# Window attention on one core: one value slot in place of two, value eviction on VectorE, and a new order of MLP input, residual sum and fourth maximum on VectorE and GpSimd

## The chip, the cores and the metric

The kernel runs on 1 core of one Trainium2 chip. The metric is the device time of one execution in microseconds (us). Three executions of the kernel before took 1966.45, 1970.64 and 1970.95 us; the median is 1970.64 us.

## The reference

Two layers work on x, float32 of shape 8 x 48 x 112 x 112. The change touches the first alone: attention in shifted windows of 7 x 7 tokens, 3 heads of 16 channels, then an MLP of 192 hidden channels.

```python
xn = layernorm(x over channels); xs = roll(xn, (-3, -3))
xw = xs as windows of 49 tokens                       # 2048 windows
q, k, v = split(xw @ qkv_w + qkv_b)                   # 3 heads of 16
attn = softmax(q @ k.T * 16 ** -0.5 + bias)
out = (attn @ v) @ proj_w + proj_b
x = x + roll(out back to the image, (3, 3))
h = gelu(layernorm(x) @ fc1_w + fc1_b)
x = x + (h @ fc2_w + fc2_b)
```

The second layer (a 7 x 7 depthwise convolution, a normalisation, an MLP with a response norm and a residual) follows in the same launch. Its code is the same before and after.

## The kernel before

**Tiling.** `attention_phase` goes through 64 strips. A strip is two rows of 16 windows, one on partitions 0 to 48, one on partitions 64 to 112: 784 columns of 48 channels and a row of ones. A strip's attention is done in 4 quads (j = 0 to 3) of 4 windows of each partition half, so 8 windows together.

**Keys, values and scores.** `u_product` multiplies a strip's normalised input with each head's query-key matrix; the result `Uf` (float32) and its low part `Ul` (bf16) hold, in `UV` slots of 784 columns, three heads and behind them the value weights. `keys_and_values` (L931) then uses the tokens of a window as weights and lets the slots of `Uf` and `Ul` pass: one product gives a window's 3 x 49 scores and its values in one row of PSUM tile `ps_t`, `SV` = 49 `UV` columns. Before, `UV` is 5: two slots hold the value weights, once with the columns of the upper half and once with those of the lower (`wv`, `wv_swap`), so that 96 value columns come out with zeros in place of the other half's channels. `key_bias` (L944) and `shift_scores` (L959) add the bias and subtract the maximum.

**Eviction.** On ScalarE, `exp_scores` (L716) writes the exponentials of a quad to `P` and `keep_values` (L725) copies its value columns to `V`, 113 x 384 at a time; both have two buffers. `weigh` (L973, L978) multiplies `P` with `V` and with ones, `invert_sums` (L733) and `invert_sums_end` (L740) give the reciprocals of the sums, and `divide` (L522, VectorE) writes `O`. `project` (L987) multiplies `O` with `proj_w`.

**After attention.** `first_residual` (L533, VectorE) adds the input and gives `x1`, in two halves; `x1_low` (L441, GpSimd) takes its low part; `centre` (L848) sums the channels, `subtract_mean` (L543), `square`, `variance` (L848), `log_variance` and `root` give the scale; `normalise1` (L551, VectorE) gives `xh1`, the MLP's input, `low1` (L406, GpSimd) its low part. `fc1` (L1009) in three parts, `gelu` (ScalarE) and `fc2` (L1022, L1028) follow, and `second_residual` (L563, VectorE) writes the result.

**Order.** Each engine runs a list written out by hand, `step(s)`, that mixes four strips: `s` (attention), `prv` = s - 1 (last quads, projection, first residual), `old` = s - 2 (MLP), and `nxt`, `nx2` (input). Semaphores count what is done. TensorE's order in a step is: quad 0 of `keys_and_values`, `variance(old)`, `weigh(prv, 3)`, `u_product(nxt, 0)`, quad 1, `project(prv)`, `weigh(s, 0)`, `u_product(nxt, 1)`, quad 2, `u_product(nxt, 2)`, `weigh(s, 1)`, `centre(prv)`, quad 3, `fc1(old, 0..2)`, `weigh(s, 2)`, `fc2(old)`, with the query scores of later quads between them.

**Banks.** Projection, centring, `u_product`, `fc1` and `fc2` share the three banks of `ps_m`. `BANKS` says which: `"proj": (1, 2)`, `("u", 1): (0, 1)`, `("u", 2): (2, 0)`. So `u_product(nxt, 1)` writes bank 1, which `project(prv)` filled just before, and waits until the first half of `first_residual(prv)` has read it; `u_product(nxt, 2)` waits so for the second half.

```python
mm(bank("proj", b)[0:R, 0:HALF], proj_w[:], O[:, s.slot(2), cols_of(b)],
   start=True, stop=True).then_inc(S["proj"], 1)
taken("proj", b, S["x1_made"], 2 * s.n + b + 1)
```

**Start.** Ahead of the first strip ScalarE spreads the value weights over both rings of `Uf` in eight copies (L800), and GpSimd takes their low parts in two instructions of 1568 columns (L460). `keys_and_values` of the first quad waits for these.

## Time and profile before

| | before |
|---|---|
| three executions, median | 1970.64 us |
| profiled execution, its own time | 1975.34 us |
| its span, first to last instruction | 1973.7 us |
| TensorE busy | 1772.9 us, 90% |
| ScalarE busy | 1541.7 us, 78% |
| VectorE busy | 1365.0 us, 69% |
| GpSimd busy | 1170.0 us, 59% |
| mean granted TensorE clock | 0.951 |

The span has three stretches: the attention phase from the start to about 1378 us, the convolution to about 1625 us, the second MLP to the end. The profiled execution took 4.70 us more than the median of the three; 1.64 us of its time lie outside the span. Busy shares are means over the whole span, so what bounds the attention phase has to be read from the timeline of one strip. In a timeline row an instruction's successor on the same engine often starts some 0.08 us before the recorded end.

### The profile page before, as it was taken

To read this page: it belongs to the slowest core of one execution; us is meant where nothing else is said; L and a number is where in the kernel's file an instruction comes from. 1 tells how busy PE (TensorE), PEld (TensorE's weight loads), DVE (VectorE), ACT (ScalarE), POOL (GpSimd) and SP (SyncE) were. 2 spreads that over 40 slices of the span, in tenths; PEclk is the share of its full clock that TensorE was granted. 3 is DMA by queue.
4 is the path that set the end of the run, shared out by engine and by line. 5 is a ranking of instruction groups with operands and counts; after the bars stand their busy time and mean duration, and the time that the engine had idled before them with its cause. 6 is when DMAs were issued, how large, how long until landed. Compare 5 with 4: busy or idle time off the path is not lost. (4 is left out here: it accounts for less than half of the span.)

```text
span 1973.7 us, 90330 instructions
## 1 busy us (share of the span) xinstructions
PE 1772.9 (90%) x38186; PEld 1076.4 (55%) x38186; DVE 1365.0 (69%) x2016; ACT 1541.7 (78%) x2904; POOL 1170.0 (59%) x1048
## 2 busy tenths in 40 slices
PE   4999999999999999999999998995899967999996
PEld 2666556656565565655666565651497943333332
DVE  7776666767676676766767676642777766888883
ACT  3788788888888788888888888873766647888882
POOL 5687686777778677777877777652255550122222
PEclk9999999999999899999999999996799985999998
DMA  4344554444444344444444444411488759999994
GB/s 111 94 108 99 139 129 103 105 102 110 100 113 102 96 107 100 116 99 105 106 107 103 104 112 99 98 45 43 109 216 216 214 135 170 227 253 253 262 258 147
DMA packets 233228, 262.26 MB, mean 133 GB/s; under 512 B 167079, under 2 KB 179911, under 8 KB 232711
## 3 DMA queue, kind: packets, MB, share of 16 engines
q1 hardware_dynamic: 217478, 217.50, 46.2%
q0 software_dynamic: 15360, 39.08, 6.6%
q8 instruction: 304, 4.98, 1.1%
q14 instruction: 86, 0.70, 0.1%
HBM read 160.82 MB, written 80.88 MB: 122 GB/s over the span
## 5 line engine op out<-in xcount | busy, mean ns | idle before, releaser
L416 POOL TENSOR_TENSOR shift<-const_b,qmax 113x588 bf16<-113x588 bf16 x256 | 299.4, 1170 | 231.8 <-DVE qmax L511 230.1
L563 DVE TENSOR_TENSOR x<-ps_m,x 112x392 f32<-112x392 f32 x128 | 66.5, 561 | 272.8 <-PE ps_m L1028 272.8
L511 DVE TENSOR_REDUCE qmax<-ps_s 113x12 f32<-113x588 f32 x256 | 194.9, 761 | 66.8 <-PE ps_s L907 66.7
L1487 POOL DMA_DIRECT2D out_rolled<-r_OUT x128 | 63.8, 503 | 270.2 <-DVE r_OUT L1587 270.2
L716 ACT ACTIVATE P<-ps_t 113x588 f32<-113x588 f32 x256 | 172.0, 672 | 58.4 <-PE ps_t L959 57.1
L748 ACT ACTIVATE G<-ps_m 128x392 f32<-128x392 f32 x384 | 178.3, 500 | 46.0 <-PE ps_m L1009 45.5
L503 DVE TENSOR_TENSOR Ul<-Uf 113x784 bf16<-113x784 f32 x192 | 208.5, 1113 | 0.0
L1333 PE MATMUL conv_ps<-xin,band_now 64*64 64x448 bf16 x2688 | 203.1, 364 | 2.2 <-DVE x_low L1228 2.2
L406 POOL TENSOR_TENSOR xhl<-xh 113x784 bf16<-113x784 f32 x64 | 200.7, 3137 | 2.2 <-DVE xh L551 2.2
L709 ACT COPY Uf<-ps_m 113x392 f32<-113x392 f32 x384 | 172.9, 486 | 33.0 <-PE ps_m L874 24.8
L1333 PE MATMUL conv_ps<-x_low,band_now 64*64 64x448 bf16 x1344 | 179.6, 351 | 0.0
L973 PEld LDWEIGHTS ps_o<-P,V 113*32 113x32 f32 x6144 | 109.1, 110 | 99.3 <-ACT P L716 53.0
L522 DVE TENSOR_TENSOR O<-ps_o,rden 96x196 f32<-96x196 f32 x256 | 90.0, 352 | 89.5 <-ACT rden L740 84.0
L1333 PEld LDWEIGHTS conv_ps<-xin,band_now 64*64 64x64 bf16 x2688 | 136.2, 105 | 22.9 <-issue 3.9
L973 PE MATMUL ps_o<-P,V 113*32 113x49 f32 x6144 | 143.2, 211 | 4.2 <-issue 0.6
L441 POOL TENSOR_TENSOR xl<-x 113x784 bf16<-113x784 f32 x64 | 137.0, 2141 | 12.1 <-DVE x L533 7.0
L733 ACT ACTIVATE lden<-ps_o 96x196 f32<-96x196 f32 x256 | 84.5, 330 | 74.4 <-PE ps_o L978 65.8
L978 PE MATMUL ps_o<-P,pack 113*32 113x98 f32 x3072 | 136.6, 250 | 0.1
L1201 POOL DMA_DIRECT2D y_scratch<-y x96 | 67.9, 708 | 112.6 <-ACT y L1272 105.9
L389 POOL TENSOR_TENSOR t_cen<-XT,t_mean 112x672 f32<-112x672 f32 x64 | 126.3, 1973 | 10.9 <-DVE t_mean L482 10.9
L1624 ACT ACTIVATE r_G<-r_ps_f 128x784 f32<-128x784 f32 x128 | 104.6, 839 | 28.5 <-PE r_ps_f L1694 28.4
L725 ACT COPY V<-ps_t 113x384 f32<-113x384 f32 x256 | 125.0, 488 | 1.9 <-PE ps_t L959 1.9
(244 smaller groups left out, 5203.9 us busy)
## 6 DMA issues: line engine op xcount, KB each, us to landing
xin<-rows_scratch SPq DMA_DIRECT2D x96, 236.0 KB, 3.8
XT<-x_tokens SPq DMA_DIRECT2D x64, 294.0 KB, 3.3
X<-x_windows SPq DMA_DIRECT2D x128, 147.0 KB, 3.4
RS<-rs_scratch SPq DMA_DIRECT2D x128, 147.0 KB, 3.4
XR<-x_windows SPq DMA_DIRECT2D x128, 147.0 KB, 3.2
x_scratch<-x SPq DMA_DIRECT2D x128, 147.0 KB, 3.4
y_scratch<-y POOLq DMA_DIRECT2D x96, 196.0 KB, 2.9
r_RS<-rs_scratch SPq DMA_DIRECT2D x128, 147.0 KB, 4.6
```

The source lines that it names most:

```text
L389: nc.gpsimd.tensor_tensor(t_cen[:].rearrange("p (t c) -> p t c", c=C), XT[:, s.slot(2), :].rearrange("p (t c) -> p t c", c=C), mean, ALU.s ...
L406: nc.gpsimd.tensor_tensor(xhl1[:], xh1[:], xm1[0], ALU.subtract).then_inc(S["lo1"], 1)
L416: nc.gpsimd.tensor_tensor(shift[:, j % 2], e, m, ALU.mult).then_inc(S["md"], 1)
L441: nc.gpsimd.tensor_tensor(xl1[:], x1[:, r, :], x1m[0][:, r, :], ALU.subtract).then_inc(S["x1_lo"], 1)
L503: nc.vector.tensor_tensor(Ul[:, r, h, :], Uf[:, r, h, :], U[0][:, r, h, :], ALU.subtract).then_inc(S["u_lo"], 1)
L511: nc.vector.tensor_reduce(qmax[:, j % 2, :].rearrange("p (b n) -> p b n", b=2), ps_s[0:R, :, 0:2 * HQ].rearrange("p b (n t) -> p b n t", t ...
L709: nc.scalar.copy(Uf[:, s.slot(2), h, cols_of(b)], bank(("u", h), b)[0:R, 0:HALF]).then_inc(S["u_hi"], 1)
L716: nc.scalar.activation(P[:, j % 2].rearrange("p (b n) h t -> p b n (h t)", b=2), ps_t[0:R, :, 0:2 * SV].rearrange("p b (n c) -> p b n c", ...
L748: nc.scalar.activation(out, bank(("f1", k), b)[:, 0:HALF], ACT.Gelu).then_inc(S["ge"], 1)
L973: mm(ps_out[lo:lo + 2 * DH, TOK * k:TOK * k + TOK], V[:, j % 2, k, lo:lo + 2 * DH], P[:, j % 2, k, h, :], start=True, stop=True)
L978: ins = mm(ps_den[lo:lo + 2 * DH, 2 * TOK * b:2 * TOK * (b + 1)], key_ones[:, b ^ j // 2, :], P[:, j % 2, 2 * b:2 * b + 2, h, :], start=Tr ...
L1333: ins = mm(ps[s][SIDE * k:SIDE * k + SIDE, side, 0:half * IMG], band_now[lo:lo + SIDE, s, w, t, :], part[lo:lo + SIDE, s, half * k:half * ...
```

## The change

1. `UV` becomes `HEADS + 1`. One slot holds the value weights of both halves, so the moving side of each L931 product is 4 x 49 = 196 columns and no longer 245. `wv_swap` goes; the setup copies to `Uf` become two, of 784 columns, and GpSimd's low parts two of 784.
2. A product now gives 48 value columns for each half, without zeros. `V` is laid out as [row, quad parity, window, channel, half]; VectorE evicts a quad with two copies of 49 partitions x 192 columns, one for each half of the partitions, each writing every second word. The places of the other half are cleared once, on GpSimd. ScalarE's four `keep_values` in a strip go.
3. The copies of quads 0 and 1 wait for ScalarE's exponentials of the same quad, those of quads 2 and 3 come first and the exponentials wait for them.
4. For quads 2 and 3 the windows of a quad are taken in another order, and `O` and `proj_w` are laid out to fit: `project` makes two products as before, of windows by kind and not by half, and `first_residual` reads and writes 4 x 98 columns in place of 392 running ones.
5. VectorE's order: `normalise1(old)` moves ahead of `first_residual(prv)`, `query_max(s, 3)` behind it, and the four `keep_values` are put in. GpSimd's order: `low1(old)` goes ahead of `x1_low(prv)`, and `make_shift(s, 3)` behind both.

```diff
-        UV = HEADS + 2
+        UV = HEADS + 1
...
-        V = sb("V", [R, 2, QP, 2 * C])
+        V = sb("V", [R, 2, QP, C, 2])
...
-        O = sb("O", [2 * C, 2, STRIP])
+        O = sb("O", [2 * C, 2, 2, QUADS, 2 * TOK])
...
+        def kept_values(p, j):
+            lo = ROWB * p
+            to = V[lo:lo + TOK, j % 2, :, :, p].rearrange("p (b k) c -> p b k c", b=2)
+            of = ps_t[lo:lo + TOK, :, 0:2 * SV].rearrange("p b (k c) -> p b k c", c=SV)[:, :, :, HQ:HQ + C]
+            return to, of
...
                 make_shift(s, 2)
+                low1(old)
+                x1_low(prv)
                 make_shift(s, 3)
-                x1_low(prv)
-                low1(old)
...
+            def keep_values(s, j):
+                if s.real:
+                    q = 4 * s.n + j
+                    wait(dve, S["st"], q + 1)
+                    if j < QUADS // 2:
+                        wait(dve, S["ex"], q + 1)
+                    wait(dve, S["pv"], q - 1)
+                    for p in range(2):
+                        nc.vector.tensor_copy(*kept_values(p, j)).then_inc(S["vev"], 1)
...
                 query_max(s, 2)
+                keep_values(s, 0)
                 token_sums(s.at(4))
                 token_squares(s.at(3))
                 divide(prv, 3)
                 normalise0(nx2)
+                normalise1(old)
+                keep_values(s, 1)
+                first_residual(prv)
                 query_max(s, 3)
-                first_residual(prv)
-                normalise1(old)
                 divide(s, 0)
+                keep_values(s, 2)
...
                 divide(s, 1)
+                keep_values(s, 3)
                 query_max(nxt, 1)
...
             def exp_scores(s, j):
...
+                    if j >= QUADS // 2:
+                        wait(act, S["vev"], 2 * (q + 1))
...
-                                    w = QP * j + 2 * b + k
+                                    w = QP * j + 2 * (b ^ j // 2) + k
```

VectorE in a step, from the division of quad 2 of `prv` to that of quad 0 of `s` (`L522` before, `L542` after; `L533` and `L553` are the first residual, `L551` and `L572` `normalise1`, `L534` the new copies). Before:

```order
L522 TENSOR_TENSOR O<-ps_o,rden 96x196
L511 TENSOR_REDUCE qmax<-ps_s 113x12
L479 TENSOR_REDUCE t_sum<-XT 112x14
L482 TENSOR_SCALAR t_mean<-t_sum 112x14
L488 TENSOR_REDUCE t_var<-t_sqr 112x14
L522 TENSOR_TENSOR O<-ps_o,rden 96x196
L497 TENSOR_TENSOR xh<-X,RS 113x784
L511 TENSOR_REDUCE qmax<-ps_s 113x12
L533 SCALAR_TENSOR_TENSOR x<-ps_m,out_b,XR 113x392 x2
L551 SCALAR_TENSOR_TENSOR xh<-xc,centred_b,rs 113x784
```

The same place after:

```order
L520 TENSOR_REDUCE qmax<-ps_s 113x12
L534 COPY V<-ps_t 49x192 x2
L488 TENSOR_REDUCE t_sum<-XT 112x14
L491 TENSOR_SCALAR t_mean<-t_sum 112x14
L497 TENSOR_REDUCE t_var<-t_sqr 112x14
L542 TENSOR_TENSOR O<-ps_o,rden 96x2x98
L506 TENSOR_TENSOR xh<-X,RS 113x784
L572 SCALAR_TENSOR_TENSOR xh<-xc,centred_b,rs 113x784
L534 COPY V<-ps_t 49x192 x2
L553 SCALAR_TENSOR_TENSOR x<-ps_m,out_b,XR 113x4x98 x2
L520 TENSOR_REDUCE qmax<-ps_s 113x12
```

Ahead of the first residual two pairs of copies and `normalise1` are new, and the fourth maximum has gone behind it.

GpSimd from the shift of quad 3 on (`L416`, after `L425`; `xhl` is written by `low1`, `xl<-x` by `x1_low`). Before:

```order
L416 TENSOR_TENSOR shift<-const_b,qmax 113x588 x2
L441 TENSOR_TENSOR xl<-x 113x784
L406 TENSOR_TENSOR xhl<-xh 113x784
L389 TENSOR_TENSOR t_cen<-XT,t_mean 112x672
L416 TENSOR_TENSOR shift<-const_b,qmax 113x588
```

After:

```order
L425 TENSOR_TENSOR shift<-const_b,qmax 113x588
L415 TENSOR_TENSOR xhl<-xh 113x784
L450 TENSOR_TENSOR xl<-x 113x784
L425 TENSOR_TENSOR shift<-const_b,qmax 113x588
L398 TENSOR_TENSOR t_cen<-XT,t_mean 112x672
L425 TENSOR_TENSOR shift<-const_b,qmax 113x588
```

The low part of the MLP's input now comes first, that of the residual sum second, and the fourth shift third.

## Rows read from the trace of the kernel before

**Rows 1.** Timeline of TensorE, one strip: start us, us, line, output and inputs, count.

```profile
910.65 0.30 PE L931 MATMUL ps_t<-Uf,xh 49*49 49x245 bf16 x4
...
911.72 0.33 PE L907 MATMUL ps_s<-swap,Uf 49*49 49x49 bf16 x24
911.88 0.42 PE L959 MATMUL ps_t<-shift,const_b 49*49 49x294 bf16 x4
...
915.96 1.57 PE L987 MATMUL ps_m<-O,pack 96*113 96x392 f32 x4
...
918.28 0.36 PE L874 MATMUL ps_m<-xh,gram_h 49*49 49x392 bf16 x4
...
921.56 0.38 PE L848 MATMUL ps_m<-x,sum_w 113*113 113x392 bf16 x1
...
922.12 0.33 PE L848 MATMUL ps_m<-xl,sum_w 113*113 113x392 bf16 x1
922.40 0.30 PE L931 MATMUL ps_t<-Uf,swap 49*49 49x245 bf16 x4
...
923.48 0.32 PE L907 MATMUL ps_s<-xh,Uf 49*49 49x49 bf16 x24
923.77 0.37 PE L1009 MATMUL ps_m<-xh,w_part_h 49*64 49x392 bf16 x4
...
926.84 0.35 PE L1009 MATMUL ps_m<-xh,w_own_h 49*128 49x392 bf16 x2 [0.52 <-ACT G L748]
...
930.74 0.30 PE L931 MATMUL ps_t<-Uf,xh 49*49 49x245 bf16 x4
```

**Rows 2.** Timeline of VectorE in the same strip.

```profile
912.87 0.84 DVE L479 TENSOR_REDUCE t_sum<-XT 112x14 f32<-112x672 f32 x1
...
914.14 0.84 DVE L488 TENSOR_REDUCE t_var<-t_sqr 112x14 f32<-112x672 f32 x1
915.09 0.36 DVE L522 TENSOR_TENSOR O<-ps_o,rden 96x196 f32<-96x196 f32 x1
915.37 0.96 DVE L497 TENSOR_TENSOR xh<-X,RS 113x784 f32<-113x784 f32 x1
...
917.02 1.18 DVE L533 SCALAR_TENSOR_TENSOR x<-ps_m,out_b,XR 113x392 f32<-113x392 f32 x2
918.12 1.03 DVE L551 SCALAR_TENSOR_TENSOR xh<-xc,centred_b,rs 113x784 f32<-113x784 f32 x1
...
924.47 0.76 DVE L511 TENSOR_REDUCE qmax<-ps_s 113x12 f32<-113x588 f32 x1
```

**Rows 3.** Timeline of ScalarE in the same strip.

```profile
912.34 0.66 ACT L716 ACTIVATE P<-ps_t 113x588 f32<-113x588 f32 x1 [0.68 <-PE ps_t L959]
...
919.07 0.87 ACT L709 COPY Uf<-ps_m 113x392 f32<-113x392 f32 x2
```

**Rows 4.** Timeline of GpSimd in the same strip.

```profile
918.34 2.15 POOL L441 TENSOR_TENSOR xl<-x 113x784 bf16<-113x784 f32 x1
920.46 3.26 POOL L406 TENSOR_TENSOR xhl<-xh 113x784 bf16<-113x784 f32 x1
```

**Rows 5.** Groups of instructions: count, busy us, mean ns of one, idle before.

```profile
L1515 DVE COPY r_w1t<-r_ps_f 48x192 f32<-48x192 f32 x1 | 0.3, 342 | 0.0
L563 DVE TENSOR_TENSOR x<-ps_m,x 112x392 f32<-112x392 f32 x128 | 66.5, 561 | 272.8 <-PE ps_m L1028 272.8
L725 ACT COPY V<-ps_t 113x384 f32<-113x384 f32 x256 | 125.0, 488 | 1.9 <-PE ps_t L959 1.9
```

**Rows 6.** GpSimd's `squares_low` (L433), all 64: duration ns min/median/max.

```profile
L433 POOL TENSOR_TENSOR sql<-sq x64: 1485/1489/1498, 71.2 to 1347.7; 113x784 bf16<-113x784 f32 x64
```

**Rows 7.** Timeline of the start: GpSimd, then VectorE.

```profile
26.10 8.01 POOL L460 TENSOR_TENSOR Ul<-Uf 113x1568 bf16<-113x1568 f32 x2 [3.87 <-ACT Uf L800]
...
30.49 6.46 DVE L503 TENSOR_TENSOR Ul<-Uf 113x784 bf16<-113x784 f32 x3
```

**Rows 8.** One stretch of 20 us: busy us (count) of PE, PEld, DVE, ACT, POOL; PEclk, DMA.

```profile
220.00:240.00 20.00, 17.95 (x397) 10.85 (x399) 11.97 (x17) 13.62 (x30) 12.48 (x11) 0.83 0.38 106
```

More of the change, by code:

```diff
@@ L530, in first_residual @@
                     wait(dve, S["x2_made"], 2 * (s.n - 1))
-                    for b in range(2):
-                        wait(dve, S["proj"], 2 * s.n + b + 1)
+                    for a in range(2):
+                        wait(dve, S["proj"], 2 * s.n + a + 1)
                         nc.vector.scalar_tensor_tensor(
-                            out=x1[:, r, cols_of(b)], in0=bank("proj", b)[0:R, 0:HALF], scalar=out_b[:, 0:1],
-                            in1=XR[:, r, cols_of(b)], op0=ALU.add, op1=ALU.add).then_inc(S["x1_made"], 1)
+                            out=of_kind(x1[:, r, :], a), in0=bank("proj", a)[0:R, 0:HALF].rearrange("p (j t) -> p j t", j=QUADS),
+                            scalar=out_b[:, 0:1], in1=of_kind(XR[:, r, :], a), op0=ALU.add, op1=ALU.add
+                            ).then_inc(S["x1_made"], 1)
             def subtract_mean(s):
@@ L797, in _ @@
             for r in range(2):
[L798 to L803 removed]
+                nc.scalar.copy(Uf[:, r, HEADS, :].rearrange("p (w t) -> p w t", t=TOK),
+                               wv[:].unsqueeze(1).to_broadcast([R, WINS, TOK])).then_inc(values_spread, 1)
             steps(step, -1, N + 2)
@@ L922, in keys_and_values @@
                     wait(pe, S["ex"], q)
-                    wait(pe, S["vev"], q)
+                    wait(pe, S["vev"], 2 * q)
                     r = s.slot(2)
@@ L984, in project @@
                     wait(pe, S["nrm"], 4 * s.n + 4)
-                    for b in range(2):
-                        free_m("proj", b)
-                        mm(bank("proj", b)[0:R, 0:HALF], proj_w[:], O[:, s.slot(2), cols_of(b)],
+                    for a in range(2):
+                        free_m("proj", a)
+                        mm(bank("proj", a)[0:R, 0:HALF], proj_w[:, a, :], O[:, s.slot(2), a],
                            start=True, stop=True).then_inc(S["proj"], 1)
-                        taken("proj", b, S["x1_made"], 2 * s.n + b + 1)
+                        taken("proj", a, S["x1_made"], 2 * s.n + a + 1)
             def fc1(s, k):
@@ L1790, in constants @@
             minus[lo + j, j] = -1
-    key_ones = np.zeros((R, 2, 2 * DH), f)
+    key_ones = np.zeros((R, DH, 2), f)
     for g in range(2):
@@ L1794, in constants @@
         ones[lo:lo + TOK, lo:lo + TOK] = 1
-        for b in range(2):
-            key_ones[lo:lo + TOK, b, DH * (g ^ b):DH * (g ^ b) + DH] = 1
+        key_ones[lo:lo + TOK, :, g] = 1
     out["picks"] = np.concatenate([pick, ones, minus], 1)
-    out["key_ones"] = key_ones.reshape(R, 4 * DH)
+    out["key_ones"] = key_ones.reshape(R, 2 * DH)
     out["eye"] = np.eye(128, dtype=f)
@@ L1859, in packs_of @@
         put(a, PACK_A, "w2_part", prm0["fc2_w"][F1:HID], F2 * g)
-        for h in range(HEADS):
-            put(a, PACK_A, "proj_w", prm0["proj_w"][DH * h:DH * h + DH], 2 * DH * h + DH * g, lo)
+        for kind in range(2):
+            first = PACK_A["proj_w"].start + R * kind + ROWB * (g ^ kind)
+            a[g:2 * C:2, first:first + C] = prm0["proj_w"]
         put(a, PACK_A, "bias", by_query, lo)
```

56 lines of the change are left out of this document (19 added, 37 removed).

## The prediction

> **What bounds the kernel now.** I read the engines' totals first, then the timeline of one strip, engine by engine, then the groups of instructions. The totals name TensorE, but a mean says little; in the timeline the same strip comes back every 20.09 us, from one L931 to the next, 910.65 to 930.74 [rows 1]. Below, times are counted from 910.65. TensorE is the engine that sets the end, and the reader is to see in its rows where it runs product behind product and where it waits. It waits for the GELU in the MLP (0.52 at 16.19, and once more like it). It also waits twice by little: the last centring product starts at 11.47, its successor could start 0.17 later, yet L931 starts at 11.75, 0.11 late (behind an exponential); and the 24 score products of L907 take 0.16 at 1.07 but 0.29 at 12.83, because the MLP behind them waits for GpSimd's low part, which ends at 923.72 and lets L1009 start at 923.77 [rows 1, 4]. All else around the change hangs on this list, so I ask of each edit whether it moves a product of TensorE.
>
> **Fewer columns.** From 910.65 to 911.72 TensorE does six groups of 245 columns and three of 294, 2352 columns in 1.07 us, 0.455 ns each [rows 1]. So 49 columns less in six groups save 0.13 us a quad, 0.53 a strip, if columns are all that counts; if the groups are held by something else, nothing. I take 0.13 and keep 0 for the range. Only what no later wait eats is a gain.
>
> **ScalarE** loses 4 copies of 0.49 us a strip, 125 us in all [rows 5]. It gains TensorE nothing by itself: where ScalarE is waited for, it has itself waited for TensorE just before (0.68 us ahead of the exponential of quad 0 [rows 3], and in the GELU part the chain goes product, GELU, product). I count 0.
>
> **VectorE's copies.** No row shows this copy. The nearest is a copy of 48 x 192 out of PSUM, 342 ns [rows 5]. Since a successor starts 0.08 before the recorded end (0.36 at 915.09, successor at 915.37 [rows 2]), a pair costs 0.54 us; 2.2 us a strip, on an engine that was busy for 69% of the span. What matters is where they stand. Two pairs and `normalise1` come ahead of the first residual, the maximum goes behind it. Walk VectorE with its old durations [rows 2, 3]. The exponential of quad 0 ended at 2.35; 0.13 earlier is 2.22, and VectorE's token sums began at 2.22 as well. First pair from 2.26, token sums at 2.80 (old 2.22), squares 1.27 later at 4.07, division 0.76 later at 4.83 (old 4.44), `normalise0` at 5.11, `normalise1` 0.88 later at 5.99, second pair 0.95 later at 6.94, first residual at 7.48 (old 6.37). Its first half takes 0.63 (the pair took 1.18, so one starts 0.55 after the other): 8.11.
>
> The division's end, 5.19, lets the projection start at about 5.3, where it started before (5.31): the saving of quads 0 and 1, 0.26, is gone there. Then the bank: `u_product(nxt, 1)` started at 7.63 [rows 1] and had slack, since the residual's first half was done at 7.0. Now it starts at 8.11 and 0.1 for the signal (GpSimd to TensorE took 0.05 above): 8.21, **0.58 late**. This is a new wait, TensorE for VectorE. Behind it hang ScalarE's two copies of that product, at 8.42 before [rows 3], then the reciprocal, the division of quad 0, the second `weigh`; they were already one chain from product to centring, so centring is as late, 11.49, and the columns of quad 2 are covered by that chain.
>
> **From centring on.** Its four products take 0.73 without the old wait of 0.11 (ScalarE's exponential of quad 2 no longer stands behind a copy): L931 of quad 3 at 12.22. From there to the MLP it was 1.37; less 0.13 of columns and 0.13 of waiting for GpSimd: 1.11, so 13.33 (old 13.12). What follows to the end of the strip, 6.97, goes by GELU and stays. A strip would be 20.30. One thing more is late: VectorE came to the next strip's first maximum at 13.82 and comes to it some 1.4 later; it ends near 16.0, and the last third of `fc1`, behind scores that wait for it, wants to start at 16.4. I add 0.08 for it (0 to 0.4). **Sum: +0.29 us a strip**, over 63 strips +18.
>
> **GpSimd's order.** `low1` took 3.26 and `x1_low` 2.15, `squares_low` of the same shape always 1.49 [rows 4, 6]. The first two lie over VectorE instructions with two inputs in SBUF. `low1` now starts at about 7.1 beside copies out of PSUM; at 1.49 it ends at 8.6, `x1_low` starts at 8.8 and ends at 10.3, ahead of the centring at 11.5. So the gain is the 0.13 counted above. By the Trainium skill, "SBUF — State Buffer", section "SBUF: two separate sides", whichever of GpSimd and a VectorE instruction with two SBUF inputs starts first holds the shared ports for its whole length. The trace agrees (3.26 against 1.49). By that rule the three L503 subtractions would now run into the fourth shift and the token centring, which is one more reason for the 0.08.
>
> **Start.** GpSimd's 8.01 us for the value weights' low parts become two of about 1.5 to 2.5, and VectorE's three subtractions, 6.46 us for what takes 0.9 each elsewhere, are free of it [rows 7]. I take -4 us once (-2 to -5). Setup rows that go otherwise hide under this. The convolution and the second MLP: 0.
>
> The profiled execution took 1975.34, 4.7 above the median, and the sum of changes applies to either: 1975.3 + 18 - 4 = 1989 for it, and 1970.6 + 14 = 1985 for the median.
>
> **Rivals.** (A) As worked out: 1975 to 1998, with the columns worth 0 (+0.13 twice, +16 us) at the upper end and shorter copies at the lower.
>
> (B) The copies are slower: they write every second word, which no row of VectorE shows. Bound: a copy of 192 that costs what 392 elements cost, 561 ns [rows 5], is 0.22 longer; four of them stand ahead of the first residual: +0.88 a strip, +55, 2040. Half of that gives 2012. Against it: all PSUM reading rows here lie near one element a cycle. By the Trainium skill, "Vector Engine (DVE) Microarchitecture Reference", section 5.2, a stream is at full rate only in runs of two adjacent words, and a destination that hops every element measured 1.71 ns an element against 1.054; by its figures an estimate is 0.13 a copy, +0.5 a strip and 2018. No run here shows it yet.
>
> (C) It comes out faster. Mechanism: VectorE reaches the first residual at or before 6.9, so that the bank is free at 7.63, and TensorE runs at its own pace: centring at 10.9, L931 at 11.65, MLP at 12.76, strip 19.73, -0.36 and -23, with the start 1944. It decides at 0.58 us off VectorE's stretch from 0.3 to 8.1; that is the price of the two pairs less one copy, or 0.2 off each of the three long instructions that I walked at their old durations. For it: no row shows the copies, and my walk carries three signals at 0.04 to 0.1 each. Against: the other terms of the walk are rows.
>
> (D) A wash: half of the new wait, and the start's gain: 1965 to 1976.
>
> (E) The clock. In one stretch of 20 us it was granted at 0.83 with TensorE busy for 17.95 [rows 8]; at full clock that work would take 3 us less (17.95 x 0.17). A new wait of 0.6 us in each strip may make such stretches more or fewer; three of them either way are 10 us. It has no chance of its own and widens all cases.
>
> **How the numbers follow.** Chances: A 0.50, B 0.17, C 0.20, D 0.13. The likeliest gives 1985; its own range is 1975 to 1998. The range for 8 in 10 leaves out the lower half of C and the upper third or so of B: 1950 to 2022. About 0.3% (6 us) is what a measurement of this kernel can tell from no change. Slower by more than that: A and B, 0.66 with a little of A given to no change; same: most of D, 0.13; faster: C and a rest of D, 0.21.
>
> **What would show it.** Right: strips of about 20.3 to 20.4; L874 of the second product preceded by idle time that ends with VectorE's first residual, 0.5 us a strip; copies at about 0.34; `low1` at about 1.5; the first L931 some 4 us earlier. Wrong: copies of 0.45 or more (B), or no wait of TensorE for the residual and a strip under 20 (C); L931 groups no shorter than before, which costs A 0.13 to 0.26 a strip; or the MLP's last part waiting for a maximum, which would make the 0.08 larger.

## The result, and the profile after

| | before | after |
|---|---|---|
| median of the executions taken side by side | 1968.55 us (4) | 2209.46 us (4) |
| range | 1965.45 to 1970.95 | 2200.37 to 2212.59 |
| span of the profiled execution | 1973.7 us | 2210.9 us |
| TensorE busy | 1772.9 us | 1893.0 us |
| VectorE busy | 1365.0 us | 1567.9 us |
| ScalarE busy | 1541.7 us | 1453.9 us |
| GpSimd busy | 1170.0 us | 981.4 us |
| mean granted TensorE clock | 0.951 | 0.881 |

The changed kernel takes 1.1222 times as long, 95% interval 1.1186 to 1.1257. The prediction, 1985 us with 2022 as its upper end, had the sign right and missed the size by a factor of about 17: +241 us and not +14.

Timeline of TensorE after, one strip of 24.57 us, from one L938 (it was L931) to the next; columns as in [rows 1].

```profile
906.68 0.27 PE L938 MATMUL ps_t<-Uf,xh 49*49 49x196 bf16 x4
906.78 0.26 PE L938 MATMUL ps_t<-Ul,xh 49*49 49x196 bf16 x4
...
912.01 1.57 PE L996 MATMUL ps_m<-O,pack 96*113 96x392 f32 x4 [0.21 <-DVE O L542]
...
915.25 0.36 PE L881 MATMUL ps_m<-xh,gram_h 49*49 49x392 bf16 x4 [0.85 <-DVE x L553]
...
918.53 0.38 PE L855 MATMUL ps_m<-x,sum_w 113*113 113x392 bf16 x1
...
919.34 0.28 PE L938 MATMUL ps_t<-Uf,swap 49*49 49x196 bf16 x4
...
922.14 0.37 PE L1018 MATMUL ps_m<-xh,w_part_h 49*64 49x392 bf16 x4 [1.51 <-DVE xc L564]
...
923.87 0.56 PE L1018 MATMUL ps_m<-xhl,w_own_h 49*128 49x392 bf16 x2
...
928.04 2.57 PE L1031 MATMUL ps_m<-G,pack 128*64 128x392 f32 x8
...
931.25 0.28 PE L938 MATMUL ps_t<-Uf,xh 49*49 49x196 bf16 x4
```

The wait that was forecast is there (0.85 us ahead of L881, for the first residual). A second one, 1.51 us ahead of `fc1` (L1018), is larger and was not in the prediction. Its releaser is `xc`, which `subtract_mean` writes, and `fc1` doesn't read `xc`. What it waits for is a bank: `BANKS` has `"cen": (2, 0)` and `("f1", 0): (1, 2)`, and bank 2 comes free when the first half of `subtract_mean(prv)` has read the sums in it. In the profile's list of waits the two stand with their sum, times and longest:

```profile
PE ps_m L1018 <- DVE xc L564: 86.6, 62, 1.8
...
PE ps_m L881 <- DVE x L553: 50.4, 61, 0.8
```

Why `xc` is late is in the timelines of VectorE and, behind it, GpSimd of the same strip:

```profile
908.98 0.74 DVE L534 COPY V<-ps_t 49x192 f32<-49x192 f32 x2
909.75 0.85 DVE L488 TENSOR_REDUCE t_sum<-XT 112x14 f32<-112x672 f32 x1
910.64 0.18 DVE L491 TENSOR_SCALAR t_mean<-t_sum 112x14 f32<-112x14 f32 x1
...
914.48 1.16 DVE L553 SCALAR_TENSOR_TENSOR x<-ps_m,out_b,XR 113x392 f32<-113x392 f32 x2
...
917.20 0.36 DVE L542 TENSOR_TENSOR O<-ps_o,rden 96x196 f32<-96x196 f32 x1 [0.89 <-ACT rden L755]
917.65 0.74 DVE L534 COPY V<-ps_t 49x192 f32<-49x192 f32 x2
918.43 2.97 DVE L512 TENSOR_TENSOR Ul<-Uf 113x784 bf16<-113x784 f32 x2
921.42 1.04 DVE L564 SCALAR_TENSOR_TENSOR xc<-ps_m,x 113x392 f32<-113x392 f32 x2
```

```profile
913.87 1.49 POOL L415 TENSOR_TENSOR xhl<-xh 113x784 bf16<-113x784 f32 x1 [3.64 <-DVE xh L572]
915.78 1.49 POOL L450 TENSOR_TENSOR xl<-x 113x784 bf16<-113x784 f32 x1 [0.42 <-DVE x L553]
917.23 1.17 POOL L425 TENSOR_TENSOR shift<-const_b,qmax 113x588 bf16<-113x588 bf16 x1
918.36 1.32 POOL L398 TENSOR_TENSOR t_cen<-XT,t_mean 112x672 f32<-112x672 f32 x1
```

The kernel before, VectorE and then GpSimd (rows not shown so far):

```profile
913.74 0.49 DVE L482 TENSOR_SCALAR t_mean<-t_sum 112x14 f32<-112x14 f32 x1
...
920.24 0.36 DVE L522 TENSOR_TENSOR O<-ps_o,rden 96x196 f32<-96x196 f32 x1 [1.10 <-ACT rden L740]
920.52 1.85 DVE L503 TENSOR_TENSOR Ul<-Uf 113x784 bf16<-113x784 f32 x2
922.28 1.03 DVE L543 SCALAR_TENSOR_TENSOR xc<-ps_m,x 113x392 f32<-113x392 f32 x2
```

```profile
920.46 3.26 POOL L406 TENSOR_TENSOR xhl<-xh 113x784 bf16<-113x784 f32 x1
923.68 2.04 POOL L389 TENSOR_TENSOR t_cen<-XT,t_mean 112x672 f32<-112x672 f32 x1
```

Counted from each strip's first L938 or L931, `subtract_mean` started at 11.63 and starts at 14.74, 3.11 later. The division before it is 0.93 later (10.52 against 9.59: the first residual's delay and the longer copies). From division to the pair of subtractions for `Ul` it took 0.28 and takes 1.23, which is the copies of quad 2. The pair itself took 1.85 and takes 2.97. Before, VectorE had the pair to itself and GpSimd's `low1` waited for it, 3.26 in place of 1.49. After, GpSimd's token centring starts 0.07 ahead of the pair and ends at 919.68; from there to the pair's end at 921.40 are 1.72. So a delay of about 1.1 us that GpSimd bore before, without harm to TensorE, lies on VectorE now, ahead of `xc`. Before, the first half of `xc` was out near 12.2 (an estimate: 11.63 and 0.56 for a half), 0.9 ahead of `fc1` at 13.12. That slack is gone and `fc1` starts at 15.46.

Then the clock. Two stretches of the strip after and two of the strip before, each up to `fc1` and from `fc1` to the next strip; columns as in [rows 8].

```profile
906.68:922.14 15.46, 12.80 (x385) 9.02 (x378) 13.88 (x24) 9.41 (x21) 7.01 (x7) 1.00 0.40 96
922.14:931.25 9.11, 8.52 (x109) 3.99 (x113) 3.54 (x7) 6.67 (x12) 5.20 (x4) 0.63 0.27 69
```

```profile
910.65:923.77 13.12, 13.06 (x384) 9.20 (x377) 11.55 (x19) 10.87 (x26) 8.35 (x8) 1.00 0.47 116
923.77:930.74 6.97, 5.73 (x117) 2.82 (x112) 2.50 (x4) 6.51 (x13) 6.97 (x5) 1.00 0.36 89
```

Up to `fc1` a strip has grown by 2.34 us, all of it idle time (TensorE is busy for 12.80 and was for 13.06). From `fc1` on it has grown by 2.14 us, and there TensorE is not idle but slow: busy 8.52 in place of 5.73, the granted clock 0.63 in place of 1.00, between the levels of 1.2 and 2.4 GHz; it has run at 2.4 GHz up to a wait of 1.51 us and is granted 1.2 GHz for most of what follows it.

The strip before stands for nearly all of its kernel, the strip after for most of its own: 48 of 61 MLP parts are slow, at 8.2 to 10.5 us. The other 13 take 6.97, ten of them behind a part up to `fc1` as long as in the strip shown. Over the 61 whole strips of each profile (sums over the starts in TensorE's timeline) the part up to `fc1` sums to 806.7 us before and 935.2 after, +128.5; the part from `fc1` on to 435.1 and 538.1, +103.0. From the first `fc1` to the last it is 1276.1 against 1507.5, +231.4 of the 237.2 by which the spans differ.

### The profile page after: what moved, and what is told of

It is laid out like the page before. It is cut to its first block and busy times, and to the rows that moved or that the text cites. A ratio compares the mean times of both kernels' runs of the same rounds, so it can differ in the third digit from the quotient of the medians.

```text
span 2210.9 us, 90580 instructions
## 1 busy us (share of the span) xinstructions
PE 1893.0 (86%) x38186; PEld 1132.5 (51%) x38186; DVE 1567.9 (71%) x2526; ACT 1453.9 (66%) x2642; POOL 981.4 (44%) x1048
## 5 line engine op out<-in xcount | busy, mean ns | idle before, releaser
L425 POOL TENSOR_TENSOR shift<-const_b,qmax 113x588 bf16<-113x588 bf16 x256 | 299.9, 1172 | 312.3 <-DVE qmax L520 312.3
L512 DVE TENSOR_TENSOR Ul<-Uf 113x784 bf16<-113x784 f32 x192 | 246.5, 1310 | 2.3 <-ACT Uf L731 0.3
L415 POOL TENSOR_TENSOR xhl<-xh 113x784 bf16<-113x784 f32 x64 | 95.7, 1495 | 229.6 <-DVE xh L572 229.6
L534 DVE COPY V<-ps_t 49x192 f32<-49x192 f32 x512 | 181.6, 355 | 17.3 <-ACT P L740 2.0
L981 PEld LDWEIGHTS ps_o<-P,V 113*32 113x32 f32 x6144 | 122.0, 120 | 115.5 <-issue 63.1
L981 PE MATMUL ps_o<-P,V 113*32 113x49 f32 x6144 | 158.2, 225 | 6.6 <-DVE O L542 0.9
L1031 PE MATMUL ps_m<-G,pack 128*64 128x392 f32 x512 | 153.4, 743 | 4.9 <-ACT G L763 4.9
L987 PE MATMUL ps_o<-P,pack 113*32 113x98 f32 x3072 | 152.6, 272 | 0.0
L1342 PE MATMUL conv_ps<-x_low,band_now 64*64 64x448 bf16 x1344 | 146.1, 353 | 0.0
L542 DVE TENSOR_TENSOR O<-ps_o,rden 96x196 f32<-96x196 f32 x256 | 90.4, 353 | 66.7 <-ACT rden L755 64.8
L1342 PEld LDWEIGHTS conv_ps<-xin,band_now 64*64 64x64 bf16 x2688 | 125.6, 106 | 12.0 <-issue 4.5
L881 PE MATMUL ps_m<-xh,gram_h 49*49 49x392 bf16 x768 | 70.4, 352 | 56.7 <-DVE x L553 50.4
```

Source lines behind the costliest of these rows:

```text
L425: nc.gpsimd.tensor_tensor(shift[:, j % 2], e, m, ALU.mult).then_inc(S["md"], 1)
L512: nc.vector.tensor_tensor(Ul[:, r, h, :], Uf[:, r, h, :], U[0][:, r, h, :], ALU.subtract).then_inc(S["u_lo"], 1)
L534: nc.vector.tensor_copy(*kept_values(p, j)).then_inc(S["vev"], 1)
L981: mm(ps_out[lo:lo + 2 * DH, at:at + TOK], V[:, j % 2, k, DH * h:DH * h + DH, :], P[:, j % 2, k, h, :], start=True, stop=True)
L987: ins = mm(ps_den[lo:lo + 2 * DH, at:at + 2 * TOK], key_ones[:], P[:, j % 2, 2 * b:2 * b + 2, h, :], start=True, stop=True)
L1031: mm(bank("f2", b)[lo:lo + ROWB, 0:HALF], w2_own[:], G[:, r, g, cols_of(b)], start=True, stop=False)
```

## The experiments

In the table, "to fc1" and "MLP" are the mean length of these two parts of a strip over 61 strips, "slow" is the number of strips whose MLP part is over 7.3 us, and "clock" is the granted clock of the stretch from 200 to 1200 us. The ratio is to the kernel before, run beside it.

| kernel | median us | ratio (95%) | to fc1 | MLP | slow | clock |
|---|---|---|---|---|---|---|
| before | 1968.55 | 1 | 13.22 | 7.13 | 6 | 0.99 |
| after | 2209.46 | 1.1222 (1.1186 to 1.1257) | 15.33 | 8.82 | 48 | 0.87 |
| e4_order_only | 2072.23 | 1.0537 (1.0361 to 1.0713) | 13.98 | 7.72 | 23 | 0.95 |
| e6_copies_old_order | 2286.34 | 1.1599 (1.1552 to 1.1646) | 15.88 | 9.46 | 59 | 0.83 |
| e1_xc_early | 2095.71 | 1.0656 (1.0611 to 1.0701) | 14.49 | 7.85 | 24 | 0.95 |
| e2_tokens_early | 2065.35 | 1.0502 (1.0354 to 1.065) | 14.51 | 7.14 | 7 | 0.99 |
| e7_both_early | 2020.99 | 1.0253 (1.0205 to 1.03) | 14.02 | 7.04 | 4 | 1.00 |
| e8_cand | 2022.21 | 1.0263 (1.0221 to 1.0305) | 13.71 | 7.36 | 12 | 0.99 |
| e9_order_tokens | 1958.94 | 0.9969 (0.9946 to 0.9991) | 13.11 | 6.97 | 2 | 1.00 |
| e10_tokens_only | 1963.33 | 0.9974 (0.9959 to 0.9989) | 13.20 | 7.04 | 4 | 1.00 |
| e5_columns_only | 1976.96 | 1.0025 (0.9994 to 1.0055) | 13.36 | 7.12 | 7 | 0.99 |
| e12_columns_new_order | 1962.06 | 0.9967 (0.9948 to 0.9987) | 13.13 | 7.05 | 2 | 1.00 |
| e13_pairs_2_3 | 1985.79 | 1.0094 (1.0057 to 1.0131) | 13.41 | 7.12 | 4 | 0.99 |
| e14_pairs_0_1 | 2032.62 | 1.0313 (1.0292 to 1.0335) | 14.24 | 7.09 | 3 | 1.00 |
| e3_fill | 2256.25 | 1.1472 (1.1341 to 1.1603) | 16.15 | 8.84 | 41 | 0.93 |
| e11_two_low | 2233.72 | 1.1351 (1.1324 to 1.1379) | 15.25 | 9.24 | 61 | 0.85 |
| e15_quarter_low | 2003.56 | 1.0164 (1.0143 to 1.0185) | 13.71 | 7.11 | 7 | 0.99 |

### Is it the late centring? e1, e2, e7, e8

Theory: `xc` is late for two causes, its place behind the pair of subtractions and GpSimd's instructions beside that pair. Rival: the 0.85 us for the residual is what counts, as predicted, and the rest follows from it. `e1_xc_early` puts `subtract_mean` one place forward, `e2_tokens_early` moves GpSimd's token centring away, `e7_both_early` does both. Each is the changed kernel with:

```diff
# e1, VectorE
                 u_low(nxt, 0)
-                u_low(nxt, 1)
                 subtract_mean(prv)
+                u_low(nxt, 1)
# e2, GpSimd
                 make_shift(s, 2)
+                centre_tokens(s.at(4))
                 low1(old)
                 x1_low(prv)
                 make_shift(s, 3)
-                centre_tokens(s.at(4))
```

> The changed kernel with one move on VectorE: subtract_mean(prv) stands behind the first of the three subtractions Ul (L512) and not behind the second. Theory W (wait): fc1's first product waits 1.5 us a strip for subtract_mean, because the bank it writes holds the channel sums until VectorE has read them; with the move that wait falls to 0.3 us or less, the first fc1 product starts at about 14.0 after the strip's start in place of 15.5, and the strip loses 1.3 to 1.7 us at least (2209 to about 2110 us), up to 3.5 us if the clock recovers with it (about 1990). Rival L (the low part is what fc1 waits for, or the clock is low for a reason that no wait makes): the move brings under 0.3 us a strip, over 2190 us.

> The changed kernel with one move on GpSimd: the token centring (1.32 us) stands ahead of both low parts, where GpSimd waited 3.6 us, and no longer beside VectorE's Ul subtractions. Theory P (ports): the first Ul pair took 2.97 us in place of 1.85 because GpSimd's token centring held the shared ports; without it the pair falls to 2.2 or less, subtract_mean comes 0.8 to 1.1 us earlier and so does fc1: about 2209 - 63 x 0.9 = 2150 us, less if the clock recovers. Rival: the pair stays near 3 us, because it is slow beside the fourth shift or the copies; the time stays above 2195 us.

> The changed kernel with both single moves: token centring early on GpSimd, subtract_mean behind the first Ul on VectorE. Alone they gave strips of mostly 21.52 and 21.72 us. Theory: fc1's wait for subtract_mean is then gone altogether (it was 0.42 us in one strip of two with the token centring early), a strip is 20.09 + 0.94 for the second u_product waiting for the first residual - 0.14 columns - 0.1, some 20.8 to 21.2 us, 2010 to 2040 us, clock 0.98 or more. Rival (the two moves cure the same wait, and what is left is the maximum that the score products of the next strip wait for): 21.4 us or more, over 2050 us.

e1 gains 114 us and e2 144 us, one line each. VectorE in e2, and TensorE's `fc1`:

```profile
910.40 1.86 DVE L512 TENSOR_TENSOR Ul<-Uf 113x784 bf16<-113x784 f32 x2
912.29 1.04 DVE L564 SCALAR_TENSOR_TENSOR xc<-ps_m,x 113x392 f32<-113x392 f32 x2
```

```profile
907.22 0.36 PE L881 MATMUL ps_m<-xh,gram_h 49*49 49x392 bf16 x4 [1.04 <-DVE x L553]
913.00 0.65 PE L1018 MATMUL ps_m<-xh,w_part_h 49*64 49x392 bf16 x4 [0.42 <-DVE xc L564]
```

The gain of e2 is the less sure one, since its two executions took 2053.63 and 2077.07 us. The pair is back at 1.86 and `fc1`'s wait falls from 1.51 to 0.42, while the wait for the residual is still there, 1.04. So the rival falls: that wait was not the larger part. e7 takes the wait for `xc` away altogether and is still 2.5% slower than the kernel before. `e8_cand` also put the residual ahead of `normalise1` and `x1_low` ahead of `low1`; the wait for the residual fell to 0.23, but the shift and `low1` met the pair again (L512 from 200 to 1200 us at a mean of 1237 ns against 969 in e7), `fc1` waited 0.34 for `xc` again, and it gained nothing over e7. I had expected 1955 to 1985 us of it, so that expectation fell.

> As the run with both moves, and the first residual ahead of normalise1 on VectorE, the residual's low part ahead of the MLP input's on GpSimd. VectorE then reaches the first residual some 0.9 us earlier. Theory: the second u_product waits under 0.2 us in place of 1.04, a strip is 20.0 to 20.3 us and the kernel 1955 to 1985 us, equal to the kernel before. If the low part of the MLP input becomes the last to come (normalise1 ends at about 8.8 us after the strip's start, its low part at 11 to 12, needed at 13), nothing more is lost. Rival (VectorE's list as a whole is too long for the strip with the copies on it, whatever its order): over 2020 us.

### Order against copies: e4, e6

`e4_order_only` is the kernel before with only the two new orders (point 5 of the change), `e6_copies_old_order` is the changed kernel with only the old ones.

```diff
# e4, on the kernel before
-                query_max(s, 3)
-                first_residual(prv)
                 normalise1(old)
+                first_residual(prv)
+                query_max(s, 3)
...
                 make_shift(s, 2)
+                low1(old)
+                x1_low(prv)
                 make_shift(s, 3)
-                x1_low(prv)
-                low1(old)
```

> The kernel before with the new order alone (normalise1 ahead of the first residual, the fourth maximum behind it, low1 ahead of x1_low and the fourth shift behind both); two value slots and ScalarE's copies stay. Theory (copies on VectorE make the delay): the first residual comes 0.2 us later, inside the 0.5 us that the second u_product had to spare, so the strip stays within 0.2 us of 20.09 and the time within 1% of 1970. Rival (the order itself makes it): the token centring now falls on the Ul subtractions and delays subtract_mean by 1 us, 2020 us or more.

> The changed kernel with VectorE and GpSimd in the order of before (fourth maximum, copies of quad 1, first residual, normalise1; on GpSimd fourth shift, residual's low part, MLP input's low part, token centring). It asks how much of the loss is the order. The new order alone cost 104 us on the kernel before. Theory (order and copies are two losses that add, by the ports and by VectorE's list): 2209 less about 100, 2090 to 2130 us, with TensorE waiting for the first residual as before (0.85 us) and for the MLP input's low part, which is last on GpSimd and late by 1 us. Rival (with the copies on VectorE the old order is worse, since the low part of the MLP input then lies wholly over the Ul subtractions): 2200 us or more.

I had expected the order to be harmless, and it costs 5% by itself. VectorE of e4:

```profile
894.75 3.74 DVE L503 TENSOR_TENSOR Ul<-Uf 113x784 bf16<-113x784 f32 x2
```

The two halves of this row, each from a window that holds one of them:

```profile
894.75 1.73 DVE L503 TENSOR_TENSOR Ul<-Uf 113x784 bf16<-113x784 f32 x1
896.41 2.08 DVE L503 TENSOR_TENSOR Ul<-Uf 113x784 bf16<-113x784 f32 x1
```

GpSimd in the same stretch:

```profile
893.03 1.49 POOL L441 TENSOR_TENSOR xl<-x 113x784 bf16<-113x784 f32 x1
894.48 1.17 POOL L416 TENSOR_TENSOR shift<-const_b,qmax 113x588 bf16<-113x588 bf16 x1
895.62 2.05 POOL L389 TENSOR_TENSOR t_cen<-XT,t_mean 112x672 f32<-112x672 f32 x1
```

The pair takes 3.74, and 1.85 when alone. The 1.89 between are about what is left of the shift at 894.75 (it ends at 895.65, so 0.90) and one token centring (1.32 where it lasts shortest), less some tenths at the joints. The token centring itself shows as 2.05, so 0.73 of it is waiting, for about one of the two subtractions (0.9): shift, subtraction, centring, subtraction take turns. By the Trainium skill, "SBUF — State Buffer", section "SBUF: two separate sides", the first of GpSimd and a two-input VectorE instruction to start holds the shared ports for its whole length; the trace agrees, and it shows that this works between single instructions, so that GpSimd got in between the two halves of VectorE's pair. It does not always get in: in the kernel before, `low1` is recorded 0.06 ahead of the pair, lasts 3.26, and the pair runs ahead of it in its 1.85. e6 is the slowest of the set, and my expectation (2090 to 2130 us) fell to its rival: the old orders with the copies put `low1` and the centring beside a pair that the copies have moved (3.79 us for L512 x2), and `fc1` waits 2.33. So the copies with the old order (and the narrow products) are worse than the change as a whole, and the new order alone is a loss too.

### Repairing the order: e9, e10

`e9_order_tokens` is e4 with the token centring moved as in e2; `e10_tokens_only` is the kernel before with that move alone.

```diff
# e10, on the kernel before
                 make_shift(s, 2)
+                centre_tokens(s.at(4))
                 make_shift(s, 3)
                 x1_low(prv)
                 low1(old)
-                centre_tokens(s.at(4))
```

> The kernel before with the new VectorE and GpSimd order alone (as in e4), and with GpSimd's token centring moved up, right behind the shift of quad 2. With the new order alone the pair of subtractions u_low(nxt, 1), subtract_mean(prv) took 3.74 us because GpSimd's last shift and the token centring lay beside it, the strip 21.19 us, the kernel 2072 us. Theory (port): with the token centring away only the shift of 1.2 us is left beside the pair; the pair falls to about 2.5 us, fc1's wait for the centring goes, strips are 20.1 us and the time is 1965 to 1985. If GpSimd is late rather than in the way (the low parts now 2 us later), fc1 waits for the low part of its input instead, strips stay near 21 and the time above 2040. Rival (the order itself, not its neighbours, costs the time, through the fourth maximum behind the residual): the time stays within 1% of 2072.

> The kernel before with one move: GpSimd's token centring right behind the shift of quad 2, all else as it was. low1, the low part of the MLP's input, ended 0.05 us ahead of fc1 in the kernel before, behind two shifts and x1_low; with 2 us of token centring ahead of them it ends up to 2 us later. If GpSimd is that close to TensorE's path here, fc1 waits about 1 to 2 us, strips are 21 to 22 and the time is 2030 to 2100. If its neighbours leave it (low1 took 3.26 us beside VectorE's subtractions, 1.49 without), half of that comes back: 1980 to 2010.

e9 takes 1958.94 us, 113 less than e4, and is faster than the kernel before by 0.3%, with an interval that leaves out 1. VectorE and GpSimd there:

```profile
907.04 1.85 DVE L503 TENSOR_TENSOR Ul<-Uf 113x784 bf16<-113x784 f32 x2
908.80 1.03 DVE L543 SCALAR_TENSOR_TENSOR xc<-ps_m,x 113x392 f32<-113x392 f32 x2
```

```profile
904.01 1.50 POOL L406 TENSOR_TENSOR xhl<-xh 113x784 bf16<-113x784 f32 x1 [1.86 <-DVE xh L551]
905.46 1.50 POOL L441 TENSOR_TENSOR xl<-x 113x784 bf16<-113x784 f32 x1
906.92 3.00 POOL L416 TENSOR_TENSOR shift<-const_b,qmax 113x588 bf16<-113x588 bf16 x1
```

Now it is GpSimd's shift that waits, 3.00 in place of 1.17, for both halves of the pair, and no other engine waits for it in this stretch. In the records it starts 0.12 ahead of the pair and yet loses, where in the changed kernel the token centring started 0.07 ahead and won; margins of a tenth of a microsecond are not to be told from recorded starts. Which of the two goes first there, and why GpSimd got in between the halves in e4 and not here, stays open. My expectation for e10 fell: `low1` ended 0.05 ahead of `fc1`, and I thought 2 us of work ahead of it would be felt. It wasn't (0.9974). GpSimd, in a strip of e10:

```profile
906.21 1.32 POOL L389 TENSOR_TENSOR t_cen<-XT,t_mean 112x672 f32<-112x672 f32 x1
909.12 1.18 POOL L416 TENSOR_TENSOR shift<-const_b,qmax 113x588 bf16<-113x588 bf16 x1 [1.59 <-DVE qmax L511]
...
912.44 3.17 POOL L406 TENSOR_TENSOR xhl<-xh 113x784 bf16<-113x784 f32 x1
```

GpSimd idles there for the fourth maximum, and the centring fits into that gap: `low1` starts 9.89 us behind the strip's first L931 (902.55), where it started 9.81 behind it.

### What the narrower products are worth: e5, e12

`e5_columns_only` has one value slot and the new layouts, with the copies (two of 49 x 192 for a quad) on ScalarE at their old places, and the old orders. `e12_columns_new_order` is e5 with the orders of e9. The core of e5 on the changed kernel:

```diff
-            def keep_values(s, j):          # VectorE's list
...
+            def keep_values(s, j):          # ScalarE's list
+                    for p in range(2):
+                        nc.scalar.copy(*kept_values(p, j)).then_inc(S["vev"], 1)
```

> One value slot and the new layouts of the changed kernel, but the copies stay on ScalarE at their old places (two of 49 x 192 a quad in place of one of 113 x 384) and VectorE and GpSimd keep the order of before. It asks what the columns are worth by themselves. In the changed kernel a group of four products of 196 columns starts 0.091 us after the last one, of 245 0.114: 0.14 us a quad. ScalarE pays some 0.25 us a quad for the second copy, on its way in quad 2 alone. Theory (nothing but order and copies made the loss): L931 starts follow each other in 19.9 to 20.2 us, 1950 to 1975 us with the start 2 to 4 us earlier. Rival (fewer columns leave TensorE less busy, and its clock falls more often): a granted clock under 0.97 over 200 to 1200 us and over 2000 us.

> One value slot, the value copies left on ScalarE as in e5, and the orders of e9 (normalise1 ahead of the residual, the fourth maximum behind it, token centring early, low1 ahead of x1_low). e5 had strips of 20.37 us with fc1 0.32 us late for the centring. If e9 is right that token centring was in the way, strips come to 19.9 to 20.1 (0.13 us less for each of quads 2 and 3, where no wait follows) and the time to 1950 to 1970, a little under the kernel before. If the half-width columns only move waits, 1970 to 1990.

From the first L931 group to the L907 products went 1.07 us [rows 1]; the same way is 0.93 in the changed kernel (906.68 to 907.61), so a quad saves 0.14 us, as predicted. In time it is worth nothing that can be measured: e5 is within 0.3% of before (1977, just above the 1950 to 1975 that I expected), and e12 (1962) is no faster than e9 (1959), which has the wide products. Waits have taken the place of the saving: in e5 `fc1` waits 0.33 for `xc`, which it didn't before, and in e5 and e12 quad 3's products wait for the exponential of quad 2, which stands behind two copies on ScalarE (15.3 us in 58 waits and 14.9 us in 57; before, none of that size). That these two account for all of the saving is not shown.

### Which copies cost: e13, e14

`e13_pairs_2_3` and `e14_pairs_0_1` are e12 with two of the four pairs of copies moved back to VectorE, at their places in the changed kernel. e2 is then e12 with all four.

```diff
# e14, VectorE's list (and keep_values(s, 0), (s, 1) out of ScalarE's)
                 query_max(s, 2)
+                keep_values(s, 0)
...
                 normalise1(old)
+                keep_values(s, 1)
                 first_residual(prv)
```

> e12 (1962 us) with the value copies of quads 2 and 3 on VectorE, at their places in the changed kernel; those of quads 0 and 1 stay on ScalarE. If only the first two pairs cost time, as the prediction's walk has it (first residual late, the product behind it 0.6 us late), this is 1955 to 1970. If the third pair, which stands between the division of quad 0 and the subtractions for Ul, pushes these and the centring by 0.75 us, fc1 waits some 0.4 us and more for xc, strips are 20.5 to 20.9 and the time is 1985 to 2010, more if the shift of quad 3 then meets the subtractions.

> e12 with the value copies of quads 0 and 1 on VectorE, at their places in the changed kernel; those of quads 2 and 3 stay on ScalarE. By the prediction's walk with the pairs at their measured 0.77 us the first residual is 0.8 to 1.0 us late, TensorE waits 0.6 to 1.0 us for it ahead of the second product, strips are 20.7 to 21.1 and the time is 2000 to 2025. If the last two pairs are the cause, it is 1955 to 1975 and that wait is under 0.3.

The first two pairs cost 70.6 us (2032.62 less 1962.06, where I had expected 2000 to 2025), the last two 23.7; the sum, 94.3, is near the 103.3 of all four (e2 less e12). e14 shows the predicted mechanism by itself. TensorE:

```profile
916.99 0.36 PE L887 MATMUL ps_m<-xh,gram_h 49*49 49x392 bf16 x4 [1.04 <-DVE x L553]
```

Its part up to `fc1` is 1.11 us longer than in e12 (14.24 against 13.13). In e13 it is 0.28 longer, the pair for `Ul` starts behind the copies of quad 2, and `fc1` waits for `xc`, 0.52 in the mean of 55 strips.

### The clock by itself: e3, e11, e15

Theory: the waits bring the clock down. Rival: something else in the change does (less work for TensorE, say). `e3_fill` put four repeated query-score groups (bias and product, whose result is overwritten by the same) ahead of `fc1` in the changed kernel, so that TensorE would work while it waits.

> The changed kernel with TensorE kept busy in the wait ahead of fc1: the bias and score products of the next strip's first quad are done four times more (0.29 us each, 1.2 us in a wait of 1.5 us), to the same result. No wait is taken away. Theory C (clock): the MLP stretch behind the wait ran at a granted 0.64 and took 9.1 us where it took 7.0 before, because TensorE had stood still ahead of it; with the wait filled the granted clock over 200 to 1200 us rises from 0.87 towards 0.95 or more and the strip loses about 1.5 to 2 us: 2080 to 2115 us. Rival: the lower clock comes from the fewer columns or from all waits together and the fill changes nothing or costs its own time: 2209 us or more.

It told little, and its time, 2256 us, is above the 2080 to 2115 that I expected. The mean clock from 200 to 1200 us rose (0.93 against 0.87), but the part up to `fc1` grew by 0.82 as well, and 41 of 61 strips still have a slow MLP part: in one strip there is a wait of 0.60 in the middle of the added groups, and they take longer than what they fill. The cleaner way is a wait alone, in the kernel before, where TensorE's work stays what it is. `e11_two_low` does GpSimd's `low1` twice, `e15_quarter_low` does a quarter of it twice.

```diff
# e11; e15 has [:, 0:W] on the three operands of the added line
+                    nc.gpsimd.tensor_tensor(xhl1[:], xh1[:], xm1[0], ALU.subtract).then_inc(S["lo1"], 1)
+                    wait(pool, S["lo1"], 2 * s.n + 1)
                     nc.gpsimd.tensor_tensor(xhl1[:], xh1[:], xm1[0], ALU.subtract).then_inc(S["lo1"], 1)
...
-                        wait(pe, S["lo1"], s.n + 1)
+                        wait(pe, S["lo1"], 2 * (s.n + 1))
```

> The kernel before with low1 done twice, the second time over the same data with the same result: TensorE has the same work and fc1 waits some 1.5 to 3.2 us more for GpSimd in each strip, nothing else is late. It measures the clock by itself. If a wait of this size ahead of the MLP lowers the granted clock in what follows, the stretch from fc1 to the next strip grows from 6.97 us to about 9.3 as in the changed kernel, strips are 23.5 us or more and the mean clock falls under 0.90: 2180 us or more. If the clock's fall in the changed kernel came from something else, the stretch stays at 7.0, strips are 21.6 to 23 and the clock about 0.94: 2065 to 2150 us.

> The kernel before with a quarter of low1 (196 of 784 columns) done once more ahead of it: fc1 waits some 0.5 us longer in each strip. If a small wait costs what it is and no more, strips are 20.5 to 20.7 us, the granted clock of 200 to 1200 stays at 0.97 or more, and the time is 1995 to 2015. If the clock falls with it, the clock is under 0.93 and the time above 2060.

TensorE in e11, and two stretches of it, the strip up to `fc1` and the MLP part before:

```profile
921.89 0.37 PE L1011 MATMUL ps_m<-xh,w_part_h 49*64 49x392 bf16 x4 [2.13 <-POOL xhl L408]
```

```profile
906.59:921.89 15.30, 13.11 (x385) 9.20 (x378) 13.28 (x21) 10.42 (x24) 10.32 (x8) 1.00 0.38 84
896.19:906.59 10.40, 10.04 (x108) 4.31 (x112) 0.77 (x1) 7.05 (x13) 6.42 (x5) 0.51 0.28 77
```

A wait of 2.1 us, with all the work of the kernel before and nothing else of the change, brings the MLP part to 9.24 us in the mean, all 61 strips among the slow ones, and the kernel to 2234 us, 264 more than the kernel before beside it (1969.89). In a strip 2.03 us of that are the wait (15.25 less 13.22) and 2.11 the clock behind it. The stretch shown is one of the slowest; six MLP parts in a row, from 872.10 to 1003.63, take 8.79 to 10.40 us at a granted clock of 0.51 to 0.63. In e15 the wait is 0.56, and it costs just that: 0.49 us a strip up to `fc1`, nothing behind it, 7 slow strips where the kernel before has 6. So the theory stands, and with it the division of the changed kernel's loss into waits and clock. How large a single wait may be is not settled by these runs. e14 and e7 have 1.04 at another place of the strip and keep the clock, and so does e2 with 0.42 ahead of `fc1` besides. e1, with three waits of 0.84, 0.62 and 0.69, loses it in 24 strips. e4 has one new wait, ahead of `fc1`, of 1.01 in the mean of 49 (1.1 at most, 0.63 in the strip shown), and loses it in 23.

## Why the prediction was right and wrong

**Right.** TensorE's pitch in the narrow groups fell by 0.14 us a quad (0.13), and the gain of quads 0 and 1 was gone at the projection: 5.33, forecast 5.3. The new wait for the first residual came where the walk had it, in front of the second product, because of bank 1. `low1` and `x1_low` take 1.49 each, with the figures of `squares_low` [rows 6]. The first L938 starts at 34.79 where L931 started at 38.33, 3.5 us earlier (4 forecast), though by the first `fc1` that was lost again (88.0 against 85.0). ScalarE's relief was worth nothing: it waits for TensorE instead (its idle time ahead of the exponentials is 58 us before and 137 after). Rival B, slow strided copies, is out: 355 ns in the mean of 512 against 342 [rows 5], so 0.01 more a copy and not the 0.13 or 0.22 of that rival.

**Sizes that were off.** A pair of copies goes from start to successor in 0.77 and not in 0.54 (908.98 to 909.75 above). The 0.54 took some 0.08 of overlap off each copy of 342 (by its own rows that gives 0.52); the profile's merged row says 0.74 and the successor starts behind it, not in it. Two pairs are 0.46 more. Of the first pair's 0.23 little arrived, and by luck: the walk carried `t_mean` at its old duration, 0.49, and it took 0.18, so that the division came at 4.92 (4.83 forecast). The first residual is at 7.80 and not at 7.48, the second product at 8.57, 0.94 late, and not at 8.21. Centring (11.85) and quad 3 (12.66) follow at the distances of the walk within 0.1. The walk had it that the exponential of quad 2 no longer stands behind a copy; it waits for VectorE's, and centring to quad 3 is 0.81 and not 0.73. By its own terms the upper end of rival A is 2001 (1985 and 16), not 1998.

**The step that failed** is "From centring on", in two terms. First, its 1.11 us from quad 3 to the MLP, which measured 2.80 (919.34 to 922.14), counted columns and GpSimd, but not the bank that `fc1` takes from the centring. The walk of VectorE stopped at the first residual; had it gone on, past the copies of quad 2 and the pair for `Ul`, it would have met `subtract_mean` and its 0.9 us of slack. The prediction had found the very same mechanism for `u_product` and didn't look for it at the next reader of a bank. Second, the meeting of the subtractions with GpSimd's shift and token centring was seen and put at a share of 0.08 us; in that strip it is 1.12 (2.97 less 1.85), and moving the token centring away is worth 144 us in the changed kernel (e2) and 113 us with the order alone (e9). The prediction's "The trace agrees (3.26 against 1.49)" holds for the waiting and not for who goes first: in the kernel before, `low1` is recorded 0.06 ahead of the pair and waits for both halves.

**"What follows to the end of the strip, 6.97, goes by GELU and stays"** was the other wrong sentence: 103 of 231 us are there, in products that the clock holds and not GELU (in the strip shown the products are busy for 8.52 in place of 5.73). Rival E had the clock with no chance of its own and 10 us either way. It was priced from a single stretch of the kernel before [rows 8] and as an addition to the wait; e11 shows that it can be as large as the wait that brings it on, and e15 that a wait of half a microsecond brings none. This depends on the first error: with the waits as forecast (e14 has the predicted one alone, at 1.04) the clock would have stayed, and e14's 2033 us is what the predicted mechanism costs at its real size, still above my range.

**The late maximum** (0.08, up to 0.4) cost nothing in the changed kernel; it appears as a wait of 0.4 to 0.7 ahead of the query bias only in e1, e7 and e8, the three that move `subtract_mean` forward.

## What to carry to other kernels

When a step is moved, follow each engine's list to the end of the period, and at every instruction that empties a PSUM bank ask who takes that bank next and with how much slack; one such chain found is no sign that it was the only one. Where a GpSimd instruction and a VectorE instruction with two SBUF inputs met in these runs, one waited for the other, so ask which of the two would bear the wait, and put GpSimd's long, patient work (here the token centring, 1.3 us, needed by nobody for a while) where VectorE reads PSUM or is idle: that one line was worth 0.3% in the kernel before and 6.5% in the changed one. As an estimate from e11 (2.03 us of wait, 2.11 behind it) and e4 (0.76 and 0.59), price a new TensorE wait of one to two microseconds in each period at up to twice its length, for the clock behind it; e14 shows that it can also cost its own length alone.

## What the runs showed of the hardware

- A wait of 2.1 us in each strip took the granted clock of the MLP part behind it from 1.00 to between 0.51 and 0.63 (e11, six strips; 0.63 behind a wait of 1.51 in the strip shown of the changed kernel). One of 0.56 us at the same place left the MLP part at its old length in 54 of 61 strips (e15), as in 55 of the kernel before.
- VectorE copies of 49 x 192 float32 out of PSUM take 355 ns when they write every second word; ScalarE takes 329 ns for the same copy (e5), and 488 for 113 x 384 [rows 5].
- When VectorE and GpSimd meet on SBUF, one waits for what is left of the other, and neither only slows: 2.97 = 1.85 and the token centring's rest, 3.74 = 1.85 and a shift's rest and the token centring, less the joints; 3.00 for a shift of 1.17 that waited for both halves of a pair of 1.85 (e9).
